# Cross-attention: one key tile in four has its scores kept in DRAM between the passes; one product of the scan on VectorE

## What is computed

```
# cross-attention of layer 1: 8 heads of 64, keys = 512 latents + 8192 context rows
q = latents_normed @ Wq
k, v = split(concat(context_normed, latents_normed) @ Wkv)
p = softmax(q @ k^T / sqrt(64))          # over all 8704 keys, per head and query
x = x + (p @ v) @ Wout

# selective scan of layer 0, one step for each (128-row block, group of 2 states)
state = decay * state + B * x
y    += C * state                         # the "product" of a step
```

## Time and profile before

| | |
|---|---|
| runs | 2638.22, 2645.19, 2647.38 us (median 2645.19) |
| profiled execution | 2638.76 us, its span 2637.0 us, 1.8 us outside it |
| mean granted TensorE clock | 0.968 of full speed |
| busy share | PE 94%, DVE 68%, ACT 42%, POOL 22% |
| first pass of the cross-attention | 874 to 1331 us |
| second pass | 1331 to 1849 us |
| scan, last steps | 712 to 738 us |

### The profile page before, as it was taken

How to read it: one execution, slowest core, us unless ns; L and a number is a source line. 1 busy time by engine, 2 the same in 40 slices (tenths; PEclk the granted TensorE clock), 3 DMA queues, 4 the chain that set the end, 5 groups by cost and what they waited for, 6 DMA issues and landing times.

```text
span 2637.0 us, 33262 instructions
## 1 busy us (share of the span) xinstructions
PE 2479.6 (94%) x11618; PEld 1682.7 (64%) x11618; DVE 1802.1 (68%) x1885; ACT 1115.6 (42%) x1366; POOL 592.7 (22%) x404
## 2 busy tenths in 40 slices
PE   6999989988776999999999999999898999999998
PEld 5778877654334777777655555554586777777775
DVE  5878854499978677778866666565444766666655
ACT  2334422466344222222245555554233455455543
POOL 4555544488842211111100000000000000000000
PEclk9999999999877999999999999999798999999999
DMA  7667755622021334344233222332112265666653
GB/s 273 234 239 263 265 162 176 248 72 72 0 97 48 128 155 164 127 165 154 97 120 114 96 96 73 107 110 72 64 65 118 106 227 218 225 239 223 222 215 138
DMA packets 124238, 394.73 MB, mean 150 GB/s; under 512 B 23729, under 2 KB 39293, under 8 KB 97137
## 3 DMA queue, kind: packets, MB, share of 16 engines
q1 hardware_dynamic: 95584, 326.82, 34.5%
q10 hardware_dynamic: 28560, 66.66, 7.1%
HBM read 304.14 MB, written 89.30 MB: 149 GB/s over the span
## 4 chain that ended last, share of the span: by engine, by line
PE 79%; DVE 8%; DMA 5%; issue 3%; POOL 3%; ACT 2%; ACTq 0%; SPq 0%; DVEq 0%; POOLq 0%
PE ps L2113 18%; PE ps L2114 17%; PE ps L2115 17%; PE ps L2500 10%; PE ps L2512 9%; PE ps L2407 3%; DMA w_halves<-unit_lo 3%; DVE ps L1646 2%; POOL work L955 2%; PE ps L2766 1%; DMA x_res<-in_x 1%; POOL work L936 1%; DVE ln_st L1516 1%; DMA wT_lo<-w_halves 1%; DVE work L1646 0%
## 5 line engine op out<-in xcount | busy, mean ns | idle before, releaser
L1866 DVE TENSOR_TENSOR sums<-sums,pT 128x1024 f32<-128x1024 f32 x272 | 313.7, 1220 | 188.1 <-ACT pT L1345 187.0
L1804 DVE SCALAR_TENSOR_TENSOR peak<-ps,rs_all,peak 128x1024 f32<-128x1024 f32 x272 | 335.7, 1278 | 93.9 <-PE ps L2407 93.7
L1345 ACT ACTIVATE pT<-ps,rs_all 128x1024 f32<-128x1024 f32 x272 | 278.4, 1130 | 226.4 <-PE ps L2500 224.3
L2512 PE MATMUL ps<-pT,values 128*64 128x512 f32 x1088 | 242.5, 596 | 0.0
L2512 PEld LDWEIGHTS ps<-pT,values 128*64 128x64 f32 x1088 | 74.5, 137 | 146.5 <-issue 133.8
L2230 PE MATMUL ps<-work,ident 128*128 128x512 f32 x256 | 130.3, 640 | 35.8 <-POOL work L936 18.8
L1005 POOL TENSOR_TENSOR cT_lo<-cT_raw,cT_hi 128x512 fp32r<-128x512 f32 x60 | 77.7, 1295 | 352.0 <-ACT cT_hi L1294 352.0
L2000 DVE TENSOR_TENSOR rgu_lo<-rgu_raw,rgu_hi 128x2048 fp32r<-128x2048 f32 x64 | 143.9, 2288 | 5.1 <-ACT rgu_hi L1428 5.0
L898 POOL TENSOR_TENSOR ctx_lo<-ctx_raw,ctx_hi 128x512 fp32r<-128x512 f32 x64 | 105.6, 1650 | 128.9 <-DVE ctx_hi L1551 128.9
L1646 DVE TENSOR_TENSOR_SCAN ps<-ps,work 128x1024 f32<-128x1024 f32 x50 | 114.3, 2286 | 15.2 <-ACT ps L1217 13.2
L2500 PE MATMUL ps<-q_lo,key_hi 64*128 64x512 f32 x544 | 120.6, 439 | 0.9 <-DMA scale_rows<-sd_rows_dram 0.7
(11 more groups left out here) (470 smaller groups left out, 6376.3 us busy)
## 6 DMA issues: line engine op xcount, KB each, us to landing
rgu_raw<-in_r_gate_up SPq DMA_DIRECT2D x64, 1024.0 KB, 4.8
rd_raw<-in_r_down SPq DMA_DIRECT2D x32, 1024.0 KB, 4.9
sh_raw<-in_s_parts SPq DMA_DIRECT2D x32, 768.0 KB, 4.3
key_rows<-key_hi SPq DMA_DIRECT2D x17, 1024.0 KB, 3.9
key_rows<-key_lo SPq DMA_DIRECT2D x17, 1024.0 KB, 5.9
value_rows<-values SPq DMA_DIRECT2D x17, 1024.0 KB, 8.9
ctxT_raw<-in_ctx_T SPq DMA_DIRECT2D x16, 1024.0 KB, 6.7
ctx_raw<-in_ctx SPq DMA_DIRECT2D x16, 1024.0 KB, 8.2
```

Source lines behind the costliest of these rows:

```text
L1345: nc.scalar.activation(pT[:, i], ps[:, b:b + 2], ACT.Exp, scale=rs_all[:, bass.ds(c * KT + attend_tile(j, i)[1], 1)]).then_inc(s4_exp.sem, 1)
L1804: nc.vector.scalar_tensor_tensor(peak[:, p], ps[:, b:b + 2], rs_all[:, bass.ds(c * KT + kt, 1)], peak[:, p], ALU.mult, ALU.max).then_inc(s ...
L1866: nc.vector.tensor_tensor(sums[:, p], sums[:, p], pT[:, i], ALU.add).then_inc(s4_sum.sem, 1)
L2512: done = nc.tensor.matmul(ps[e * DK:(e + 1) * DK, 6 + p], values[:, s, kt, h * DK:(h + 1) * DK], pT[:, i, e], start=start and kt == 0, sto ...
```

## The change

For one key tile in four (key tile 3, tiles 6 and 7 of a half, `COMPUTED` = 6 and up) the scores of the first pass are made full: three pairs of matmuls in place of one. ScalarE copies them with their row scale from PSUM to `kept_rows` (2 tiles, 128x2048 float32, 1 MB), VectorE takes the maximum from there, and `SP` writes them to `kept_rows_dram`. This holds for 15 near halves and 14 far halves (`is_kept`): 29 halves, 58 tiles. In the second pass the 29 blocks of these halves compute 6 tiles; the other two are read back (`kept_back`, double-buffered), VectorE adds the shift, spread over all partitions, and ScalarE takes the exponential of that. Loads of such a block: 1 MB of scores ahead of three quarters of the keys (2 x 0.39 MB), the values (0.52 MB) and the scales. The spread shift (`shift_wide`) is made by four new pairs of matmuls and four copies in blocks 1 and 2. In the scan, step 60 leaves `FAR_STEPS`, and one output block fewer is projected ahead of step 63.

```diff
-FAR_STEPS = (3, 8, 13, 18, 23, 28, 33, 37, 41, 45, 49, 53, 57, 60)
+FAR_STEPS = (3, 8, 13, 18, 23, 28, 33, 37, 41, 45, 49, 53, 57)
...
-    return (tuple(range(BLOCK)),)
+    return (tuple(range(COMPUTED if kept_block(j) else BLOCK)),)
...
+COMPUTED = 2 * (KT - 1)
...
+def is_kept(c, half):
+
+    return not isinstance(c, int) or c < KCHUNKS - 2 - half
...
+            def store_kept(c, half, rows):
+                sp.wait_ge(*kept_out(kept_halves(c, half) * 2 + 2))
+                sp.dma_start(rows[half], kept_rows[:].rearrange("p i e n -> p (i e n)")).then_inc(kept_stored.sem, 16)
...
+                if before is not None:
+                    store_kept(c - 1, 0, before)
...
                 store_chunk(c, s, keys, rows)
+                if before is not None and not (isinstance(c, int) and c >= LATE):
+                    store_kept(c - 1, 1, before)
...
+                if scores is not None:
+                    sp.dma_start(kept_back[:, s].rearrange("p i e n -> p (i e n)"), scores[half]).then_inc(kv_loaded[s].sem, 16)
...
+            def keep_scores(c, half):
+                for i in range(COMPUTED, BLOCK):
+                    act_e.wait_ge(*peak_mm((c * 2 + half) * BLOCK + (i + 1)))
+                    if i == COMPUTED and not (isinstance(c, int) and (c, half) == (0, 0)):
+                        act_e.wait_ge(*kept_stored(kept_halves(c, half) * 16))
+                    b = peak_place(c, half, i)
+                    act_e.sem_inc(act_passed, 1)
+                    nc.scalar.activation(kept_rows[:, i - COMPUTED], ps[:, b:b + 2], ACT.Copy,
+                                         scale=rs_all[:, bass.ds(c * KT + (KT - 1), 1)]).then_inc(kept_out.sem, 1)
...
+            def spread_back(p):
+                act_e.wait_ge(*spread_mm(p + 1))
...
+                nc.scalar.activation(shift_wide(p), ps[:, 4:6], ACT.Copy).then_inc(spread_out.sem, 1)
...
+                    if from_first:
+                        nc.scalar.activation(pT[:, i], kept_back[:, s, i - COMPUTED], ACT.Exp).then_inc(s4_exp.sem, 1)
...
+                    if is_kept(c, half) and i >= COMPUTED:
+                        dve.wait_ge(*kept_out(kept_halves(c, half) * 2 + (i - COMPUTED + 1)))
...
+                        nc.vector.tensor_tensor(peak[:, p], kept_rows[:, i - COMPUTED], peak[:, p], ALU.max).then_inc(s4_peak.sem, 1)
...
+                if kept_block(j):
+                    dve.wait_ge(*kv_loaded[s](turn))
+                    if isinstance(j, int) and j == 2:
+                        dve.wait_ge(*spread_out(PAIRS))
+                    for i in range(2):
+                        nc.vector.tensor_tensor(kept_back[:, s, i], kept_back[:, s, i], shift_wide(2 * half + i), ALU.add).then_inc(kept_shifted.sem, 1)
...
-                    for ib in range(3):
+                    for ib in range(2):
                         project_rows(ib, TT - 1)
...
+                    if is_kept(c, half) and i >= COMPUTED:
+                        pe.wait_ge(*k_lo(c * PAIRS + (half * 2 + 2)))
+                        parts = [(key_hi, q_lo), (key_hi, q_hi), (key_lo, q_hi)]
...
+            def spread_shift(p):
...
+                for e in range(2):
+                    rows = slice(e * DK, (e + 1) * DK)
+                    done = nc.tensor.matmul(ps[:, 4 + e], spread_ones[rows], shift_rows[rows, p], start=True, stop=True)
```

More of the change, by code:

```diff
@@ L266, in build @@
         silu_warm = lasting("silu_warm", [P, 1])
+        bc_at = lasting.at
         bc_rows = lasting("bc_rows_sb", [P, T])
@@ L2260, in _ @@
                     pe.wait_ge(sc_read, near_steps(n))
-                    for ib in range(3):
+                    for ib in range(2):
                         project_rows(ib, TT - 1)
-            for ib in range(3, IB - 1):
+            for ib in range(2, IB - 1):
                 project_rows(ib, TT - 1)
@@ L2501, in similarities @@
                     done.then_inc(s4_sim.sem, 1)
+            def spread_shift(p):
+                if p == 0:
+                    pe.wait_ge(*s4_init(5))
+                    pe.wait_ge(*shift_ready(PAIRS))
+                else:
+                    pe.wait_ge(*spread_out(p))
+                for e in range(2):
+                    rows = slice(e * DK, (e + 1) * DK)
+                    done = nc.tensor.matmul(ps[:, 4 + e], spread_ones[rows], shift_rows[rows, p], start=True, stop=True)
+                done.then_inc(spread_mm.sem, 1)
             def weigh_values(j, s, half, tiles, start=False, stop=False):
@@ L2541, in attend_pe @@
                         pe.wait_ge(*o_saved1(1))
-                    weigh_values(j, s, half, groups[0], start, stop)
+                    weigh_values(j, s, half, range(BLOCK), start, stop)
             attend_pe(0, 1, 0, 32, start=True)
```

189 lines of the change are left out of this document (138 added, 51 removed).

## The result

| | before | after |
|---|---|---|
| median | 2643.07 us | 2614.78 us (2611.60 to 2616.77) |
| profiled execution, its span | 2638.76, 2637.0 us | 2615.69, 2614.0 us |
| busy share PE, DVE, ACT | 94, 68, 42% | 94, 71, 45% |

The ratio is 0.9897, with a 95% interval of 0.9873 to 0.9920: 27.2 us less, 21 to 34. Forecast were 2616.4 us, 28.8 less. One execution of a later run, that with one more addition, took 6411.95 us in place of 2618, for a cause that isn't known, and is left out of its ratio.

What follows compares the result with a forecast made beforehand. TensorE's full stream was taken to bound both passes of the cross-attention. The terms -57.7 + 26.7 + 5.2 - 3.0 = -28.8 us took the median from 2645.2 to 2616.4 us, range 2608 to 2636.

Steps and rivals of the forecast that it cites:

- part 2: First pass: 58 tiles get two more matmul pairs, 116 x 0.23 = 26.7 us added; late chunks allowed 0 to 3 us.
- Part 1: Second pass: 29 blocks lose tiles 6 and 7 from TensorE, 14.91 to 12.92 us each, 57.7 us gained.
- T: Start of a block of the second pass; T+n is n us after it.
- The threshold of VectorE: Second pass: above 1.87 us for one addition VectorE would set the block; the two additions per block priced at nothing.
- Stores: First pass: stores of kept scores priced at nothing, cover 2 to 4 us; the next copies can begin at G+15.6.
- G: Start of a kept group of scores (tiles 6 and 7) in the first pass; G+n is n us after it.
- Part 3: Between the passes: shift matmuls and copies use up block 2's 1.99 us, block 3's loads take 3.0 more; 5.2 added.
- Part 4: End of the scan: step 60's product moves from GpSimd to VectorE and the gate comes earlier, 3.0 us gained.
- A: Second pass becomes load-bound, TensorE waits at each block's start, kernel slower; 2671 us at 160 GB/s; chance 0.06.
- B: First pass: the store lands late; 2626 us at 250 GB/s, up to 2640; chance 0.13.
- C: Second pass: ScalarE, not TensorE, sets the block, so fewer matmuls leave it at 14.91 us; 2674 us; chance 0.02.

## Why the prediction was right, and where it was off

The sum was -28.8 us; the ratio says -27.2 and the stages of the one pair of profiles say -25.3 for what was changed. The forecast of 2616.4 lies 1.6 above the median, and that nearness is in part luck: the median of before fell by 2.1 us with a fourth run, and the first pass cost 5.7 more than forecast while the second gained 2.3 more. The mechanisms are those that the stages and the runs show; part 2 is the term whose size was most off. Step by step:

- **Part 1, 57.7 us from the second pass.** Right. Blocks went from 14.91 to 12.90, 29 x 2.01 = 58.3. The choice of 1.99 over the pure matmul time of 1.84 was needed. Its cover was right in each point that was timed: sums end at T+12.0 and the additions at T+14.3, as forecast. The loads land at T+8.6, not T+10.5. The 209 GB/s was a misreading: its window in the earlier trace rows runs on past the end of the loads, for from 1493.00 to 1494.00 the same trace has 30 GB/s and before that 236 GB/s. So 1.59 MB had landed by about T+6.7, and the extra 0.78 MB at 350 GB/s would have given T+8.9. The cover is 4.3 us and not 2.4.
- **The threshold of VectorE.** The text said that additions above 1.87 us each would set the block. With two more additions a block has 4 x 1.15 = 4.6 us of them, over the threshold's 3.7, and VectorE did set the block, but only after seven blocks. The step lacked the time by which the additions may come later before TensorE misses them (T+4.7 to T+11.4): 28 x 0.85 = 24 us became 10.3.
- **Part 2, 26.7 us in the first pass.** The term was mis-sized: 32.4. The 0.92 us per half is right: 22 steady halves are 14.92 for 14.01, and the run with one product has 14.01. What failed is "in the late chunks; there I allow 0 to 3 us". It was 5.7. The cause of most of it was written in the code, in the order of ScalarE's work in chunk 14, where a copy that waits for TensorE stands ahead of a split that TensorE needs next. I had looked at the copies' cover in a steady half, where the split comes first, and not at what is queued behind the copies in the late ones. 4.9 us of it are shown by moving the split; the rest, 0.8, is in groups that wait for VectorE's maxima (1.8 us in four waits of the run with the split ahead, 1.2 in three before), which was only read.
- **Stores.** The price of nothing was right, and so was its reason. The median of 3.9 us from issue to landing is that of the near halves. In the 11 steady far halves, of which the forecast spoke, the store lands at G+13.3 to G+13.7 (forecast G+13.4) and the next copies begin at G+16.2 (forecast G+15.6). Stores twice as large cost no steady half anything and use up this room to 0.3 us.
- **Part 3, 5.2 us between the passes.** -54.8 less 29 x -2.01 leaves 3.5, the low bound. The copies of the shift and their matmuls use up block 2's gain of 2.0 us, as said: block 2's value products end 49.9 us after the start of block 0 in both kernels. What was too high is the price of block 3's loads: the wait is 2.53 us where 3.7 was said, 1.9 more than before and not 3.0, since the extra 0.78 MB was priced between 350 and the 209 GB/s that was misread. Blocks 3 and 16, which each take 12.7 us and not 12.9, give 0.4 back. The clock behind the wait, 1.5 us in some executions, was no step of the sum.
- **Part 4, 3.0 us from the scan.** Right: 2.9 in every profile with the new scan. From the scan of step 57, the sum of step 63 starts after 23.1 us, which by the clock of before is 726.1, as written. VectorE is indeed what is late next, though it is step 62's sum that waits for it (1.16 us) and not step 63's. That this gain reaches the end isn't shown: alone it measured 2.4 with 0 inside the interval.
- **Rivals.** A needs 2 MB more per block, B, in the steady part, a store more than twice as large. C is refuted by ScalarE's 4.88 us of idle time in a block. By the rule of the Trainium skill, page "Perfetto Trace Analysis", section "Identifying the Most-Contended Engine", TensorE is to be judged by the share of the peak rate that it reaches (MFU) and by the busy share of weight loads. The prediction took only the second. It is 39.3 of 80 us in the second pass, and yet each pair that was taken away shortened the block in full, so taken alone it does not tell here that TensorE is full. The share of the peak rate was not worked out.

## What to carry to other kernels

Where an engine is full, price an added or removed instruction by the distance of starts in its own stretch, and then read, for every place where the order of work differs from the steady one, what stands behind each new instruction that waits. An overloaded second engine costs nothing until its lag reaches the place where the first waits for it, so work out how late its result may come and multiply its excess only by the blocks that are left after that. A median over stores or loads that stand in different places of a queue hides the late ones, and a rate is to be read from a window that ends with the transfer. A wait of a few us on TensorE can cost about half as much again in clock (1.5 us on top of 2.6 and of 3.4 here).

## What was not expected of the hardware

- 3.4 MB a block of loads and copies (261 to 266 GB/s in windows of 40 us) leave most of TensorE's blocks at 12.9 us; with 4.4 MB the queue reached 293 GB/s with its engines busy 0.85 of the time, and blocks mostly alternated between 14.3 and 16.0 us and did not settle at one length.
- After a wait of 2.3 to 3.5 us at block 3 TensorE's granted clock fell in some executions of the same code and not in others (0.74 over 6.5 us, or 1.00), which moved block 3 by 1.5 us; it fell after a wait of 2.41 us and did not after one of 2.53. After the wait of 3.4 to 3.9 us in chunk 14 it fell in every profile that has the wait, and in neither of the two without it.
- The same feed-forward work behind the scan took 143.1 or 145.7 us. All of the difference arises between 19 and 39 us after the scan's last gate, where most of the long ones have a lower granted clock (0.51 where the short ones have 0.63 over 13.7 us), but one has 0.63 too. What decides it stays open.
